# A decoder block on one core: the last rows of a position table are gathered into other buffers, and the tokens are read back later

## The reference

```python
x = x + attention(layernorm(x))          # gated linear attention, 16 heads
x = x + mlstm(q=layernorm(x), k=v=ctx)   # 8 heads of 32
x = x + experts(layernorm(x))            # 8 experts, top 2, width 1024
```

```python
pos_emb = rpe[hops]                      # hops: 256 x 256 indices below 2017, rpe: 2017 x 256
k_hop = einsum('bhvc,vmhc->bhvm', qh, pos_emb)
C = (qk + k_hop) * D                     # D: decay below the diagonal
h = (C / normalizer) @ vh                # then a norm per head, scaled and shifted
```

## Time and profile before

| what | us |
|---|---|
| median of 3 runs | 756.69 |
| the profiled execution, its own time | 752.56 |
| its span | 750.5 |
| PE busy in the span | 716.7 |
| GpSimd busy in the span | 444.2 |
| VectorE / ScalarE busy | 399.0 / 361.6 |

### The profile page before, as it was taken

The page is one execution under the profiler, slowest core; times in us unless marked ns, Lnnn a source line. Parts: engine busy times, 40 slices in busy tenths (PEclk is TensorE's granted clock), DMA queues, the critical chain, the costliest instruction groups (busy, mean ns, idle before and its releaser), DMA issues.

```text
span 750.5 us, 17158 instructions
## 1 busy us (share of the span) xinstructions
PE 716.7 (95%) x5856; PEld 647.4 (86%) x5857; DVE 399.0 (53%) x1000; ACT 361.6 (48%) x936; POOL 444.2 (59%) x508
## 2 busy tenths in 40 slices
PE   7899999979999999979999879999999999999996
PEld 4677777859999999978999667999999999999995
DVE  3467777675756443335999993333333333333331
ACT  2444444344766444436999444444434444353441
POOL 6777777776777777775676401445454444544442
PEclk9999999999999999999999999999999999999999
DMA  8444444443333375543998993121222222122221
GB/s 294 134 119 136 130 132 140 135 127 93 95 101 104 105 235 139 154 131 104 275 260 207 305 380 143 29 42 35 35 35 38 38 35 35 35 35 40 37 35 22
DMA packets 75812, 88.29 MB, mean 118 GB/s; under 512 B 11952, under 2 KB 66032, under 8 KB 75632
## 3 DMA queue, kind: packets, MB, share of 16 engines
q0 software_dynamic: 19824, 43.93, 23.8%
q1 hardware_dynamic: 52256, 40.11, 17.9%
q10 hardware_dynamic: 3680, 3.54, 1.4%
HBM read 75.82 MB, written 11.73 MB: 117 GB/s over the span
## 4 chain that ended last, share of the span: by engine, by line
PE 77%; DVE 8%; issue 6%; POOL 4%; ACT 2%; DMA 2%; SPq 0%; DVEq 0%; POOLq 0%; ACTq 0%
PE ps L1747 19%; PE ps L1755 18%; PE ps L2053 10%; PE ps L1031 5%; POOL G L332 4%; PE ps L485 4%; PE ps L1287 2%; PE ps L552 2%; PE ps L526 2%; PE ps L478 2%; PE ps L450 1%; PE ps L1736 1%; PE ps L576 1%; PE ps L1289 1%; DMA U<-in_sw 1%
## 5 line engine op out<-in xcount | busy, mean ns | idle before, releaser
L332 POOL DMA_INDIRECT G<-in_rpe,hopi x193 | 189.7, 983 | 59.1 <-issue 52.7
L1812 ACT ACTIVATE G<-ps,U 128x128 f32<-128x128 f32 x312 | 84.9, 383 | 161.2 <-PE ps L1747 161.2
L1747 PEld LDWEIGHTS ps<-G,QT 128*128 128x128 f32 x1248 | 145.2, 192 | 1.9
L1747 PE MATMUL ps<-G,QT 128*128 128x128 f32 x1248 | 145.5, 275 | 0.0
L1755 PE MATMUL ps<-G 128*128 x624 | 141.0, 379 | 0.0
L1755 PEld LDWEIGHTS ps<-G 128*128 128x128 f32 x624 | 115.6, 190 | 14.1
L2053 PE MATMUL ps<-U,PET 128*128 128x128 f32 (+3 forms) x768 | 100.7, 275 | 0.0
L2053 PEld LDWEIGHTS ps<-U,PET 128*128 128x128 f32 x768 | 94.4, 194 | 0.1
L979 DVE COPY PET<-ps 128x512 f32<-128x512 f32 x64 | 44.2, 691 | 85.2 <-PE ps L1031 83.5
L1693 POOL DMA_INDIRECT out<-G,slots x39 | 71.4, 1830 | 23.9 <-issue 23.9
L2096 ACT ACTIVATE PET<-ps 128x512 f32<-128x512 f32 (+1 forms) x63 | 37.4, 594 | 84.7 <-PE ps L1031 81.2
(11 more groups left out here) (241 smaller groups left out, 1230.8 us busy)
## 6 DMA issues: line engine op xcount, KB each, us to landing
G<-run_max SPq DMA_DIRECT2D x16, 512.0 KB, 7.0
U<-in_w SPq DMA_DIRECT2D x16, 512.0 KB, 7.5
G<-in_w SPq DMA_DIRECT2D x8, 1024.0 KB, 12.6
G<-in_rpe,hopi POOLq DMA_INDIRECT x193, 3.0
U<-in_ctx SPq DMA_DIRECT2D x8, 256.0 KB, 2.8
tokens_kept<-X SPq DMA_DIRECT2D x8, 256.0 KB, 2.1
X<-tokens_kept SPq DMA_DIRECT2D x1, 2048.0 KB, 11.2
hidden_rows<-QT ACTq DMA_DIRECT2D x8, 256.0 KB, 7.3
```

The costliest lines, as they stand in the source:

```text
L332: pool.indirect_dma_start(out=dst, out_offset=None, in_=rpe_d, in_offset=bass.IndirectOffsetOnAxis(ap=hopi[:, n:n + 1], axis=0)) \
L1747: mm = pe.matmul(bank(1 + 2 * u + c // 4, 4, P)[:, c % 4], w1c[u][:, k, c], hT[u][:, k, :], start=(k == 0), stop=(k == KC - 1))
L1812: ins = nc.scalar.activation(gel[u][:, c, :], bank(1 + 2 * u + c // 4, 4, P)[:, c % 4], ACT.Gelu, bias=b1c[u][:, c:c + 1])
```

## The change

The change has three parts. (1) Of the last 21 columns, the first 16 (236 to 251) go into the 16 token rows of X a second time, and the last 5 (252 to 256) into slots 65 to 69 of G; for the 16, the last reader is now pair 63 to 70 instead of pair 107 to 115. (2) X is read back after `turned` >= 126 instead of 71, and stands behind the context's loads on SyncE. (3) The even pace ends 18 pairs ahead of the last pair instead of 6.

```diff
             elif n < NFIRST + NAGAIN + NBUF:
                 k = n - NFIRST - NAGAIN
+            elif n < NFIRST + NAGAIN + NBUF + NKEPT:
+                return X[:, n - NFIRST - NAGAIN - NBUF, :]
             else:
-                k = THIRD_AT + n - NFIRST - NAGAIN - NBUF
+                k = THIRD_AT + n - NFIRST - NAGAIN - NBUF - NKEPT
             return G[:, k * D:(k + 1) * D]
...
-            return NFIRST + NAGAIN + THIRD_AT + n - NFIRST - NAGAIN - NBUF
+            if n < NFIRST + NAGAIN + NBUF + NKEPT:
+                return NFULL + n - NFIRST - NAGAIN - NBUF
+            return NFIRST + NAGAIN + THIRD_AT + n - NFIRST - NAGAIN - NBUF - NKEPT
...
             context(0)
             context(1)
+            read_until(NFIRST + NAGAIN + NBUF + NKEPT - 1)
+            sp.dma_start(X[:, 0:NKEPT, :], kept_dram).then_inc(x_ld, 16)
             sp.wait_ge(prod, products_done(NPAIR - 1))
...
                 sp.dma_start(m_dram, r_M).then_inc(r_dma, 16)
-                sp.wait_ge(turned, (NFIRST - 1) // 2 + 1)
-                sp.dma_start(X[:, 0:NKEPT, :], kept_dram).then_inc(x_ld, 16)
                 sp.wait_ge(r_dma, 16)
...
-                    evenly = NTURNED + 1 + i * (NPAIR - LEAD - NTURNED) // len(rest)
+                    evenly = NTURNED + 1 + i * (NPAIR - 3 * LEAD - NTURNED) // len(rest)
```

## The result

The changed kernel takes **761.03 us** (median of 5 runs, 760.54 to 761.94), the kernel before beside it 757.05 us (5 runs, 755.54 to 758.25). The ratio is 1.0061, with a 95% interval of 1.0043 to 1.008. That is slower by 0.61%, twice what a measurement of this kernel can tell from no change. 760.2 us was predicted.

What follows compares the result with a forecast made beforehand. The chain ran over TensorE, then GpSimd's gather pace and TensorE's waits for landings. Late gather +2.6 and low clock +0.9, the rest 0, gave +3.5 us on a median of 756.69: 760.2 us, range 756.0 to 763.0 us.

Steps and rivals of the forecast that it cites:

- Parts 1 and 3: New buffers and pace for GpSimd's last gathers: they only lower counts GpSimd waits for, 0 us (bounds -4.5 and 0).
- Rival 2: `turned` counts hold GpSimd's gathers behind column 132; part 1 or 3 frees them: up to -4.5 us, 752.2 us; chance 0.10.
- Giving up the early load: Load of X at 260.61 us removed: it delayed gathers, but TensorE was over twenty pairs behind, so 0 gained.
- The load is issued as pair 125's turn ends: SyncE, position stage's end: load of X issued at about 338.3 us, the moment of column 255's gather.
- Which gather is late: Last two gathers: column 256 lands late, at 345.6 us; column 255 lands between 341.1 and 344.3 us, adding nothing by itself.
- The price of a gather under the load: Landing time of column 256 behind the load of X: 6.0 us, bounds 2.8 and 6.7 us.
- +2.6 us that was given to pair 128's: TensorE's last turn, pair 128, waits for column 256 until 345.6 instead of 343.04 us: +2.6 us (bounds 0 and +3.2).
- The low clock: TensorE's idle time ahead of pair 127 drops the clock to 0.50, slowing products behind it: +0.9 us (bounds 0 and +2.0).
- The wait at the weight: GpSimd's wait at L1219 still ends with the small loads, X landing at 349.5 us: 0, bound above +1 us.
- The sum: Whole kernel: 0 - 0 + 2.6 + 0.9 = +3.5 us, all on the path; 760.2 us.
- Rival 1: Load hardly disturbs the last two gathers, column 256 1 to 2 us late: +0.5 to +1.5 us, 757.7 us; chance 0.30.
- The signs: Load within 0.3 us of pair 125's turn; column 256 landing 5.5-6.7 us; wait ahead of pair 128; gathers and weight wait unchanged.

Runs made afterwards that it cites:

- a harmless load: Changed kernel with the load of X issued behind the last turn (129 turned pairs), against the kernel before: 756.03 us, ratio 0.9996.
- the load at 118: Kernel before with only the load of X moved, behind the context's loads held to 118 turned pairs: 756.13 us, ratio 1.0002.
- the first four experiments: Against the kernel before: new pace alone 755.11 us; load at pair 126 alone 761.32; load at pair 118 alone 756.13; changed kernel, load behind last turn, 756.03.
- the kernels made for that: Unread matmuls ahead of late turns, added to the changed kernel (ratio 1.0259) and the kernel before (1.0054), second chip; the first again on the third, 1.0273.
- the quarter kernel: Kernel before with 4 of X's 16 token rows (512 KB) read back at pair 126: 815.16 us, ratio 1.0002; third chip 814.59 us, 0.9995.

## Why the prediction was right, and where a size was off

- **Parts 1 and 3, nothing.** Right on a chip like that of the result: the 125 gathers take 163.14 us in both profiles, the pace alone gives 0.9989 with an interval over 1, and with both parts and a harmless load the ratio is 0.9996. Rival 2, that the counts hold GpSimd, had its condition met on the other two chips, but with the opposite sign: there (tried on one of them) the change lost 10.9 us.
- **Giving up the early load, 0.** Right as far as it can be told: with the load at 118 the ratio is 1.0002.
- **The load is issued as pair 125's turn ends.** Right, 0.03 us behind it. It was put at the moment of column 255's gather and came 0.55 us ahead of it, because the wait ahead of pair 125 was 1.92 us in place of 2.29.
- **Which gather is late.** The step "column 255 is issued with the load, whose data take a while to start, so it lands between 341.1 and 344.3 us" and "adds nothing by itself" failed. That the load's data take a while to start is so, but the gather's rows take a while too, 1.4 us and more behind its issue, and the argument left this out. No row bore on such a gather either: the landings behind the earlier trace rows are those of four gathers, issued at 262.3 to 266.1 us, 1.7 to 5.5 us behind their load, and the fifth, 0.4 us behind it, has no landing in the trace. Column 255 took the full delay, 6.8 us, and the wait is ahead of pair 127 and not 128. Column 256, issued 1.25 us later, was in by about 349 us, ahead of pair 128's turn, and cost nothing of its own. The price of a gather under the load, 6.0 us with 6.7 as the bound, was nearly right; it was charged to the wrong column. Pair 127's turn is 3.51 us late, against +2.6 us that was given to pair 128's (bound +3.2). Pair 128's turn is 351.18 - 343.04 - 3.38 = 4.76 us late, of which 1.25 us are the clock.
- **The low clock, +0.9 us.** Too small, the upper bound of 2.0 us was the better value: 1.82 us between pair 127's turn and the first scores. The idle time had been put at some 2 us and was 3.96 us, and the clock was at 0.50 from 344 to 352 us. It did not fall behind this wait, as had been thought, but had fallen ahead of it and stayed low.
- **The wait at the weight, 0.** Right: it ends with the small loads, 3.47 us against 3.56 before. The load itself landed in 9.4 us, not in 11.2.
- **The sum.** +3.5 us was forecast, the medians say +4.0 us, and the tail of the two profiles says +5.3. The interval of the ratio goes from +3.3 to +6.1 us, so it holds both and doesn't tell them apart; the load alone costs 4.75 us by its medians. Both terms of the sum were too small. That it still came within 0.5 us of the medians is partly luck, since they show less than the tail. The kernel before spreads over 6 us in its runs on one chip, the kernels with the late load over 1 to 1.5 us. The spread goes with the granted clock of the whole execution, 0.995 in the fastest run of before (753.47 us) and 0.984 in the slowest (759.59 us). In the profiles of before, of the changed kernel and of the first four experiments it lies ahead of the last gather, which is issued at 339.56 to 344.27 us, while from the first scores to the end it is 403.3 to 404.2 us in all six. Why the kernels with the late load spread less was not found.
- **Rival 1** falls: column 255 took 6.8 us against 2.8 in the changed kernel, and with the load alone pair 127 was turned 6.92 us behind its issue. The rule of the Trainium skill named with it (DMA: Bandwidth & Descriptors, Queues, rings and completion order: each engine goes round its queues, one packet at a time) would give about a microsecond, by the prediction's estimate from it. The trace doesn't agree: in 344 to 346 us the gathers' queue moved no packet at all. Whether its rows stood ready by then no run shows.
- **The signs.** Three held: the load issued within 0.3 us of the end of pair 125's turn, 0.30 us ahead of each gather, the wait at the weight ended by the small loads. The wait ahead of pair 128 did not come, it was ahead of pair 127. Column 256's landing stands in no row. The gathers start 3.38 us later and not within 1 us, for the reason above and not by the change.

What the runs show is that on this chip the place of the load is the whole loss, as far as the intervals tell: alone it makes it, at 118 or behind the last turn it does not. That 3.5 us of the tail are the landing and 1.8 the clock is read from the profiles. No run held the one still while the other moved; the kernels made for that met chips where neither occurs.

## What to carry to other kernels

When a large load is moved, look up which small transfers are issued within a few microseconds behind it, and how many steps are left for whoever waits for them: with six pairs left the delay took the place of later waits, with one left it was paid in full and the clock stayed low behind it. Count a transfer that was issued just ahead of the load's data, too. A load whose reader comes late can be issued when the last of the small transfers has been used. And a wait that looks idle on one chip may be what another one lives by: measure a retimed kernel on more than one before trusting tenths of a per cent.

## What was not expected of the hardware

- Three chips gave the same program 756.6, 815.0 and 815.3 us. On the third, TensorE has 16 us and more of "issue" in this stage; even the bottleneck is another, TensorE in place of the gathers. As far as the quarter kernel's profile there stands for it, all of the 58 us lies ahead of the first scores: from there to the end it takes 811.9 - 407.97 = 403.9 us, as on the first chip.
- A gather of 128 KB issued 0.55 us behind a load of 2 MB is delayed by 4 us, as much as those issued 1.7 to 5.5 us behind such a load. For 2 us and more the load alone moved data, and then the rows of two gathers came together, beside it.
- The start of the program ran at the lower clock in one profiled execution and at the full clock in the other, and behind it all stands 3.2 us later, almost the size of the effect under study. What made the difference is not shown.
